# The attention loop of a decoder layer on one core, with its side work placed anew by one table

## The reference

```python
def _L0_xattn_ref(query, key, value, wq_w, wq_b, wk_w, wk_b, wv_w, wv_b, wo_w, wo_b):
    D_MODEL, NHEAD, HEAD_DIM = 256, 16, 16
    ...
    scores = jnp.einsum('bhqd,bhkd->bhqk', Q, K) * scale
    causal = jnp.tril(jnp.ones((S, S), dtype=bool))
    scores = jnp.where(causal, scores, -jnp.inf)
    attn = jax.nn.softmax(scores, axis=-1)
    out = jnp.einsum('bhqk,bhkd->bhqd', attn, V)
    out = out.transpose(0, 2, 1, 3).reshape(B, S, D_MODEL)
    return out @ wo_w.T + wo_b
...
x = _layernorm(x + _L0_attn_ref(x, ...), axis=-1)
x = _layernorm(x + _L0_xattn_ref(x, ctx_1024, ctx_1024, ...), axis=-1)
x = _layernorm(x + _L0_ffn_ref(x, ...), axis=-1)
```

## Time and profile before

| | |
|---|---|
| median of three runs | 804.26 us |
| the profiled execution, its own time | 805.26 us |
| its span (first to last instruction) | 803.5 us, granted TensorE clock 0.888 |
| PE busy | 605.9 us, 75% |
| DVE busy | 368.8 us, 46% |
| ACT busy | 274.3 us, 34% |
| POOL busy | 197.1 us, 25% |
| chain that ended last | PE 60%, DVE 15%, DMA 9% |

### The profile page before, as it was taken

The page is one execution under the profiler, slowest core; times in us unless marked ns, Lnnn a source line. Parts: engine busy times, 40 slices in busy tenths (PEclk is TensorE's granted clock), DMA queues, the critical chain, the costliest instruction groups (busy, mean ns, idle before and its releaser), DMA issues.

```text
span 803.5 us, 11892 instructions
## 1 busy us (share of the span) xinstructions
PE 605.9 (75%) x3942; PEld 345.6 (43%) x3942; DVE 368.8 (46%) x791; ACT 274.3 (34%) x458; POOL 197.1 (25%) x253
## 2 busy tenths in 40 slices
PE   4799999998377877977876887782029999999900
PEld 2558585847143434433532453441004555555500
DVE  3654443422374645354444645515943333333526
ACT  2151414141035453554444544530004333333204
POOL 1242221210221211021110311111023444442316
PEclk9899999999569999998999999976559999999955
DMA  7890000103220422123211246004707999999254
GB/s 232 285 369 25 0 0 0 35 18 106 86 85 13 123 80 85 54 88 99 88 64 62 90 131 233 7 0 158 324 20 273 403 396 395 399 404 403 41 157 172
DMA packets 40274, 120.63 MB, mean 150 GB/s; under 512 B 3584, under 2 KB 25776, under 8 KB 36912
## 3 DMA queue, kind: packets, MB, share of 16 engines
q1 hardware_dynamic: 34928, 113.44, 37.6%
q0 software_dynamic: 4608, 6.29, 3.8%
q10 hardware_dynamic: 704, 0.47, 0.2%
HBM read 96.07 MB, written 22.02 MB: 147 GB/s over the span
## 4 chain that ended last, share of the span: by engine, by line
PE 60%; DVE 15%; DMA 9%; issue 6%; ACT 6%; SPq 1%; POOL 1%; ACTq 0%; DVEq 0%; POOLq 0%
PE PS L1778 10%; PE PS L1490 7%; PE PS L1499 7%; DMA arena<-pieces 5%; PE PS L1574 4%; DVE Mx L1009 3%; PE PS L1810 3%; PE PS L1791 3%; PE PS L1658 3%; PE PS L1645 3%; PE PS L1615 2%; PE PS L1566 2%; PE PS L1478 2%; PE PS L1461 2%; DMA sums<-row 2%
## 5 line engine op out<-in xcount | busy, mean ns | idle before, releaser
L1009 DVE TENSOR_REDUCE Mx<-PS 128x1 f32<-128x384 f32 (+3 forms) x176 | 107.5, 638 | 95.4 <-PE PS L1615 93.8
L1340 ACT ACTIVATE arena<-PS 128x512 f32<-128x512 f32 (+1 forms) x176 | 86.5, 564 | 98.3 <-PE PS L1645 98.2
L735 POOL TENSOR_SCALAR_AFFINE_SELECT arena<-arena 128x512 f32<-128x512 f32 x64 | 40.8, 637 | 225.2 <-ACT arena L1340 225.2
L1611 PE MATMUL PS<-causal,identb 128*128 128x128 bf16 (+2 forms) x176 | 46.5, 264 | 46.1 <-DVE Mx L1009 25.0
L1645 PE MATMUL PS<-arena 99*128 99x512 bf16 (+3 forms) x256 | 57.4, 316 | 16.1 <-ACT arena L1327 10.8
L1615 PE MATMUL PS<-arena 96*128 96x128 bf16 (+3 forms) x256 | 69.0, 326 | 0.0
L1490 PE MATMUL PS<-arena 128*128 128x512 f32 x128 | 55.9, 593 | 3.2 <-ACT arena L1255 1.6
L1499 PE MATMUL PS<-arena 128*128 128x256 f32 x256 | 55.9, 379 | 0.0
L1611 PEld LDWEIGHTS PS<-causal,identb 128*128 128x128 bf16 x176 | 17.5, 99 | 86.4 <-DVE Mx L1009 55.9
L1175 DVE TENSOR_TENSOR X<-PS,Y 128x512 f32<-128x512 f32 x48 | 31.0, 686 | 49.8 <-PE PS L1791 49.7
L1407 ACT ACTIVATE X<-X 128x512 f32<-128x512 f32 x48 | 29.4, 630 | 66.6 <-DVE X L1175 66.6
(11 more groups left out here) (191 smaller groups left out, 998.3 us busy)
## 6 DMA issues: line engine op xcount, KB each, us to landing
ring_a<-experts SPq DMA_DIRECT2D x12, 2048.0 KB
arena<-experts SPq DMA_DIRECT2D x12, 2048.0 KB, 18.5
ring_a<-experts SPq DMA_DIRECT2D x12, 512.0 KB
sums<-zrow SPq DMA_DIRECT2D x3, 2048.0 KB, 20.1
arena<-pieces SPq DMA_DIRECT2D x32, 192.0 KB
arena<-experts SPq DMA_DIRECT2D x12, 512.0 KB, 19.2
arena<-pieces SPq DMA_DIRECT2D x32, 128.0 KB
pieces<-arena SPq DMA_DIRECT2D x4, 768.0 KB, 3.7
```

What stands on the lines that cost most here:

```text
L735: pool.affine_select(out=pb[j % 2][:, :, 0:P], in_=pb[j % 2][:, :, 0:P], compare_op=ALU.is_ge, fill=0.0, base=0, pattern=[[0, GH], [1, P]] ...
L1009: dve.tensor_reduce(Mx[:, g % 2, i, heads[0]:heads[-1] + 1], bank((g * NSH + u) % 2)[:, 0:len(heads) * w] .rearrange("p (h n) -> p h n", h ...
L1340: act.activation(pb[j % 2][:, heads[0]:heads[-1] + 1, 0:w], bank(2 + n % 3)[:, 0:len(heads) * w] .rearrange("p (h n) -> p h n", h=len(heads)),
L1611: pe.matmul(o[:, 0:len(heads) * w].rearrange("p (h n) -> p h n", h=len(heads)) [:, :, i * P:w], identb[:], wide(causal[:], len(heads)), st ...
```

## The change

1. **The loop is a batch.** A pass is groups 0 to 3 of one batch. The first and the last pass stand outside the loop, which is left with two turns; on SP all passes are written out.
2. **One table** (`TASKS`) takes the place of three, with four places in a slot. The new first one stands amid the slot's shifted products, behind the second of them (`MID`), on PE, ACT and DVE alike. An entry names the task, its half, and the batch: 1 the next, -1 the one before, 0 this one. By groups, on PE: group 0 has value 1, query_in 0 and 1, heads 1, query 0 and 1; group 1 has split_q, key 0 and 1, split_k, output 0 and 1, stats; group 2 has norm, value 0, turn 0 and 1; group 3 has heads 0 (of its own batch) and logits. The side work for the last batch that is left behind the loop has one `heads` fewer.
3. **Banks.** Scores use banks 0, 1, 2; shifted products 3 and 4.
4. **Shares** (`CUTS`): slot 0 has all its 3 scores between the shifted products, slot 1 all 4, slot 2 has 3 there and 1 behind.
5. **The first S of a group** waits for the first copy of L1327, and the third for the second copy; before, the first waited for both.
6. **SP**: the queries' pieces go out ahead of the keys', the next tokens' transfer stands ahead of the groups' transfers, and the stores of a finished batch between those of group 1 and group 2.
7. **The end**: arrays 2 and 3 come in eight transfers of 512 KB, a batch's part each, the first of a batch behind the second layer of pair 18+b, the second behind the first layer of pair 20+b. `join` waits for its own batch.

```diff
-CUTS = [(2, 3), (2, 3), (0, 4), (0, 0)]
+CUTS = [(3, 3), (4, 4), (3, 4), (0, 0)]
+MID = 2
...
-PREPARE = {
...
-    (1, 1): ([("key", 0)], [("key", 1)], [("query", 0)]),
-    (1, 2): ([("split_k", 0)], [("query", 1)], []),
...
+TASKS = {
...
+    (1, 1): ([("key", 0, 1)], [], [("key", 1, 1)], []),
+    (1, 2): ([("split_k", 0, 1), ("output", 0, -1)], [], [], []),
...
+        score_banks, exp_banks = (0, 1, 2), (3, 4)
...
@@ -528,10 +518,10 @@
 
                 for g in kq_in:
                     sp.wait_ge(g.s, g.before(b, NRD))
+                sp.wait_ge(qsd.s, qsd.now(b, KT + 1))
+                sp.dma_start(pieces_v[1], qp).then_inc(q_out.s, 16)
                 sp.wait_ge(ksd.s, ksd.now(b, KT + 1))
                 sp.dma_start(pieces_v[0], kp).then_inc(k_out.s, 16)
-                sp.wait_ge(qsd.s, qsd.now(b, KT + 1))
-                sp.dma_start(pieces_v[1], qp).then_inc(q_out.s, 16)
 
             def group_in(b, g):
...
+            for b in range(B - 1):
+                context_in(b + 1)
-                for g in range(1, NG):
+                for g in (0, 1):
                     group_in(b + 1, g)
-                if more:
-                    context_in(b + 2)
-                    outputs(b)
-
-            with sp.Fori(0, B - 2) as b:
-                relay(b)
-            relay(B - 2, more=False)
+                if b > 0:
+                    outputs(b - 1)
+                for g in (2, 3):
+                    group_in(b + 1, g)
             weights(0, 0, second=False)
             sp.wait_ge(vpr.s, vpr.now(B - 1, 2))
+            weights(3, 3)
             outputs(B - 2)
-            for n in range(2):
-                sp.wait_ge(y2m.s, y2m.now(NP - RING - 1 + n, 1))
-                sp.dma_start(apart_sums[n], sums_all[2 + n]).then_inc(apart_in, 16)
+            for b in range(B):
+                tiles = slice(b * TT, (b + 1) * TT)
+                sp.wait_ge(y2m.s, y2m.now(NP - RING + b, 1))
+                sp.dma_start(apart_sums[0][:, tiles, :], sums_v[2, b]).then_inc(apart_in[b], 16)
+                sp.wait_ge(h1m.s, h1m.now(NP - RING + b + 2, 2))
+                sp.dma_start(apart_sums[1][:, tiles, :], sums_v[3, b]).then_inc(apart_in[b], 16)
...
                 shares = SCORED[j] if then is not None else ([], [], [])
-                maxima(then, shares[0])
+                of = len(SHARED[j])
+                half = len(shares[0]) * min(MID, of) // of
+                maxima(then, shares[0][:half])
+                dve_do(steps[0])
+                maxima(then, shares[0][half:])
                 if j == 0 and prev is not None:
                     divide(*prev)
-                dve_do(steps[0])
+                dve_do(steps[1])
                 maxima(then, shares[1])
-                dve_do(steps[1])
+                dve_do(steps[2])
                 maxima(then, shares[2])
                 if j == 2 and then is not None:
                     negate(*then)
-                dve_do(steps[2])
+                dve_do(steps[3])
 
             spare_banks[:] = 2, 3
...
                     group_out(*prev)
-                exponentials(b, g, j)
-                act_do(steps[0] + steps[1])
+                for n in exponentials(b, g, j):
+                    if n == min(MID, len(SHARED[j])):
+                        act_do(steps[0])
+                act_do(steps[1] + steps[2])
                 if j == TT - 1 and then is not None:
                     minus_max(*then)
-                act_do(steps[2])
+                act_do(steps[3])
...
 
-                    if u >= 2 or g > 0:
-                        pe.wait_ge(mxs.s, mxs.now(b, NSH * g + u - 1))
+                    if u >= 3 or g > 0:
+                        pe.wait_ge(mxs.s, mxs.now(b, NSH * g + u - 2))
                     else:
-                        pe.wait_ge(mxs.s, mxs.before(b, NSH * NG + u - 1))
-                    o = bank((g * NSH + u) % 2)
+                        pe.wait_ge(mxs.s, mxs.before(b, LAST_IN_BANK[u]))
+                    o = bank(score_banks[(g * NSH + u) % 3])
                     pe.matmul(o[:, 0:len(heads) * w].rearrange("p (h n) -> p h n", h=len(heads))
...
                 w = T - j * P
-                if j == 0:
-                    pe.wait_ge(nte.s, nte.now(b, 2 * g + 2))
                 for n, heads in enumerate(SHARED[j], FIRST[j]):
-
-                    if n >= 3:
-                        pe.wait_ge(exq.s, exq.now(b, g * NSH + n - 2))
-                    elif g > 0:
-                        pe.wait_ge(exq.s, exq.now(b, (g - 1) * NSH + (10, 11, 9)[n]))
+                    if j == 0 and heads[0] % 2 == 0:
+                        pe.wait_ge(nte.s, nte.now(b, 2 * g + heads[0] // 2 + 1))
+
+                    if n >= 2 or g > 0:
+                        pe.wait_ge(exq.s, exq.now(b, g * NSH + n - 1))
                     else:
-                        pe.wait_ge(exq.s, exq.before(b, (NG - 1) * NSH + (10, 11, 9)[n]))
+                        pe.wait_ge(exq.s, exq.before(b, NG * NSH + n - 1))
                     for a, h in enumerate(heads):
-                        mm = pe.matmul(bank(2 + n % 3)[:, a * w:(a + 1) * w],
+                        mm = pe.matmul(bank(exp_banks[(g * NSH + n) % 2])[:, a * w:(a + 1) * w],
                                        KTs[0:SX, g * GH + h, j * P:(j + 1) * P],
                                        QTs[0:SX, g * GH + h, j * P:T], start=True, stop=True)
...
                 shares = SCORED[j] if then is not None else ([], [], [])
+                of = len(SHARED[j])
                 for n, _ in enumerate(shifted(b, g, j)):
-                    of = len(SHARED[j])
                     scores(then, shares[0][n * len(shares[0]) // of:
                                            (n + 1) * len(shares[0]) // of])
+                    if n + 1 == min(MID, of):
+                        pe_do(steps[0])
                 if j == 0 and prev is not None:
                     heads_out(*prev)
-                pe_do(steps[0])
+                pe_do(steps[1])
                 scores(then, shares[1])
-                pe_do(steps[1])
+                pe_do(steps[2])
                 if j == TT - 1 and then is not None:
                     minus_max(*then)
                 if j > 0:
@@ -1715,7 +1708,7 @@
                 scores(then, shares[2])
                 if j == TT - 1:
                     values(b, g, j)
-                pe_do(steps[2])
+                pe_do(steps[3])
 
             spare_banks[:] = 2, 3
```

95 lines of the change are left out of this document (41 added, 54 removed).

## The result

| | before | after |
|---|---|---|
| median time | 805.12 us (four runs, 802.74 to 807.20; 804.26 was that of the first three) | 736.12 us (733.09 to 738.36) |
| profiled execution, own time | 805.3 us | 738.36 us |
| its span | 803.5 us | 736.1 us |
| attention loop | 304.7 us | 242.1 us |

The ratio of the two is 0.9137, with an interval of 0.9106 to 0.9167. The new kernel is faster by 69 us. The profiled execution of the new kernel is the slowest of its four.

A forecast was written before the change was run, and what follows sets the result against it. It took the loop to be bound by PE's work plus the places where its queue stands. Savings of 51.9 (loop), 0.9 (behind it) and 3.4 (end) off 805.3 gave 749.1, 748 on the median; range 737 to 771.

The forecast's parts named there:

- the allowance: In the loop, 0.4 us for each of some 30 tasks standing in three queues, 12 in all, for unseen waits.
- The walk: Step-by-step timing of the loop's groups with their tasks, a best case: 240.8 us against 304.7, 63.9 less.
- the other bounds: Fast bounds of the smaller terms: 1 us saved behind the loop, 4.4 at the end.
- the first rival: Loop: the tasks only move and holes stay empty; 34.8, 0.9 and 1.4 us saved, 768 on the median; 24%.
- The groups: Middle pass of the loop, groups 0 to 3: 17.0, 17.6, 14.3 and 13.3 us, 62.2 together.
- DVE in group 1: In group 1 DVE becomes the later engine, split maxima at 15.8; the bank of output 1 late by 0.9 us.
- The transfers: Loop: next score comes 18.8 us behind the keys' store in a middle pass; a wait of 1.2 counted once.
- Behind the loop: One turn of heads fewer on the chain behind the loop: 0.9 us saved, between 0 and 1.
- The end: Scatter chain at the end: scatter 17 little over 5 us instead of 11.7; 3.4 saved, between 0 and 4.4.
- Tasks only move: Rival, loop: each engine's queue blocks at the new places as at the old; 768 us on the median; 24%.
- Exponential banks as the bound: Rival, loop: each of 176 banks of S waits for a round trip; at 0.4 each, 70 us, 818; 3%.
- The clock: Rival: passes miss pieces, or clock stays at 0.93 in every group; 4 us a pass, 12 in all, 760; 14%.

The follow-up runs named there:

- e5_old_places: The new kernel with the tasks in their old places and the keys' store ahead of the queries' as before; 786.82 us, ratio 0.9765.
- e1_two_loads: The new kernel with arrays 2 and 3 loaded as before, in two transfers of 2 MB; 738.95 us, ratio 0.9191.
- e6_before_small_loads: The kernel before with arrays 2 and 3 loaded in eight small transfers as in the new one; 803.26 us, ratio 0.999.
- e9_after_again: The new kernel, unchanged, run again; median 735.19 us.

## Why the prediction was wrong

**The mechanism was right, the allowance was not.** The failed step is "0.4 for each, as long as the bare group's wait for a maximum, is 12". The walk gave 240.8 us for the loop; it took 242.1. So the 30 tasks lost 1.3 us together and not 12. That is a balance: the first pass came out 2.0 under the walk, the other three 0.6, 1.6 and 1.1 over it, 3.3 together where the allowance had put 9. The reason is in the pair of windows above: PE idles 3.8 us in the whole third pass, and 2.0 of it are the holes of L1636, 1.1 waits for a bank of the transposes and 0.6 the wait for the split, all three of them kinds that the walk had. Of the 3 more us a pass nothing is to be seen. My reading, which no run isolates, is that the allowance counted twice: a task that is a little late while PE has other work costs nothing, and the waits on which the path does run were in the walk already. The walk itself was the better likeliest value here.

**The range.** Its fast end was wrong by its own terms. The walk alone (63.9 off the loop) with 0.9 and 3.4 gives 736.1 on the median, and with the other bounds, 1 and 4.4, 735.0. The stated 737 cut that off; the measured 736.12 is at the first of the two. In the first rival 34.8, 0.9 and 1.4 give 767, not 768.

**The groups.** Forecast 17.0, 17.6, 14.3 and 13.3; the third pass has 17.4, 17.8, 14.4 and 13.2, and the second 18.4 in its first. The first pass took 63.2 (65.2 walked): its first group has a clock of 0.87 instead of the 0.77 taken over, which no part of the change explains, and no piece came late, though 1.2 was counted. The last took 52.3 (51.2 walked).

**DVE in group 1.** I said that DVE becomes the later engine there, with its split done at t = 15.8. In the second pass t = 0 is at 304.94, and DVE's timeline ends thus:

```profile
318.45 0.68 DVE L1037 TENSOR_TENSOR ring_a<-PS,X 128x512 f32<-128x512 f32 x1
319.05 0.68 DVE L996 TENSOR_REDUCE Mx<-PS 128x1 f32<-128x512 f32 x1
...
320.86 0.18 DVE L1014 TENSOR_TENSOR nst<-Mr,nst 128x16 bf16<-128x16 f32 x1
```

The split is done at 16.1. PE's output 1 runs until 321.1, so nothing waits for DVE; the next wait is for bank 7, as walked, but of 0.27 instead of 0.9:

```profile
319.20 1.95 PE L1559 MATMUL PS<-wo_s,Y 128*128 128x256 f32 x8
...
322.06 0.44 PE L1620 MATMUL PS<-identb,nst 128*3 128x128 bf16 x5 [0.27 <-DVE ring_a L1037]
```

**The transfers.** The keys' pieces are stored at 318.56, t = 13.6 as walked:

```profile
318.56 0.36 SPq L524 DMA_DIRECT2D pieces<-arena  x1
```

The first score of the next batch comes at 337.73, 19.2 behind it (walked: 18.8), and waits for nothing; no score of the loop waits for pieces. How close they came is not shown, as the trace has no landing time for them. In *e5_old_places* the last pieces are stored later, at t = 27.5 of the same group, and miss all three times.

**Behind the loop** it is 24.9 before and 22.7 after to the first load of the next stage: 2.2 less, forecast 0.9. What of the 1.3 more is due to the banks and what to the shorter last group was not tried.

**The end** gave 1.2 instead of 3.4. The large load's price was right (12.1 against 5.4), but I let the chain catch up with the experts right behind it. It did so only at scatter 22, the first that waits for rows of DVE; 19 to 21 stand beside small loads too, came 6.2 to 6.7 apart and waited 4.5 to 4.9 for the scatter ahead to land. *e1_two_loads* has it at 0.2, *e6_before_small_loads* at 2.2 in the profile and at nothing that its median could show. So it lies between 0 and some 2, and the sum has 1.2 from one pair of profiles.

**The sum.** Loop 62.6, behind it 2.2, end 1.2, 1.3 by which the loop begins sooner and 0.2 behind the last loads; the total of 67.4 (with roundings) is that of the spans, 803.5 to 736.1. The start is chance and no part of the change: in the new kernel the first copy ended at 223.4 in one profile and at 218.4 in the other. So the loop gave 10.7 more than forecast, the end 2.2 less, and what is behind the loop 1.3 more.

**The rivals.** Tasks only move: no; but it is just what *e5_old_places* does (moved waits at the split, 787). Exponential banks as the bound: no, one wait in 12 of 16 groups, 9.6 us in all. The clock: in this profile it is 1.00 in every group but the first; in *e9_after_again* it also falls to 0.51 where group 1 of the first pass ends (below). The Trainium skill's rule (TensorE: Matmul & The Clock Gate, "A second HAM failure mode: psum-queue depth-cycling"), under which bank cycling with short idles should make it swing, does not agree with this trace: PE passes five banks in turn (as many as before, and not more as I had written), with a wait of 0.6 to 1.1 us for an exponential in 12 of 16 groups, and behind these the clock stays.

**Not tried by themselves** were the shares of the scores, the order of the two stores, and the wait for the first copy in the new kernel. The shares and the wait are in the 18 us that *e5_old_places* leaves, the stores in the 51.

## What to carry to other kernels

Where several engines work through orders fixed in advance, first look at what stands ahead of the instruction that frees another engine: moving one 1.2 us step behind the maxima was worth 11.5 us here, and all the placing 51 of 69 (with the new place amid the shifted products). When each wait of a group has been walked with durations from a trace, take the walk itself as the likeliest value and set an allowance for the unseen only into the range (it was 1.3 us off in 241 here, the one case tried); a quick test is whether the walk leaves the fullest engine any idle time to lose. A wait costs more than its length where the clock falls behind it.
